# Mixture layer of a two-layer transformer: rows' low part moved from GpSimd to VectorE, normalising from VectorE to ScalarE

## What is computed

```
h = layernorm(x)                                   # (x - mean) / sqrt(var + eps), per row of 256
logits = (h @ router_w.T + router_b).reshape(T, O, E)
w, sel = top_k(softmax(logits, -1), 2); w = w / w.sum(-1)
c[t, e] = sum over o of the weights of expert e    # [T, 8]
out = sum over e of c[t, e] * (h @ expert_w[e].T + expert_b[e])
```

## Time and profile before

| | |
|---|---|
| median of 3 runs | 1158.56 us (1158.07 to 1158.87) |
| the profiled execution | 1155.52 us |
| its span | 1153.8 us |
| VectorE busy over the span | 854.3 us (74%) |
| TensorE, ScalarE, GpSimd busy | 981.7, 498.0, 307.6 us |
| the mixture layer | from about 287 to 597 us |

### The profile page before, as it was taken

One profiled execution on the slowest core, in us unless ns is written; L12 is line 12 of the kernel. 1 busy time (PEld: TensorE's weight loads), 2 busy tenths in 40 slices (PEclk: granted clock), 3 DMA queues, 4 the chain that ended last, 5 costly groups with the idle time before them and its releaser, 6 DMA issues. The chain is left out here.

```text
span 1153.8 us, 19875 instructions
## 1 busy us (share of the span) xinstructions
PE 981.7 (85%) x6885; PEld 579.3 (50%) x6960; DVE 854.3 (74%) x1556; ACT 498.0 (43%) x972; POOL 307.6 (27%) x337
## 2 busy tenths in 40 slices
PE   3698989897789778797649799999978999999997
PEld 1444545454446344454214366575846555656564
DVE  5677776651999999999977875858762776777766
ACT  2154444453465464564624433416131444444443
POOL 3234343441352432423321121304044400000000
PEclk9799999998899989798769999999988999999999
DMA  6622222200101001001000010101011000000000
GB/s 176 118 75 77 72 82 67 74 2 4 44 0 47 1 1 45 0 1 46 1 17 3 10 30 8 31 2 32 8 36 39 20 1 19 1 18 0 19 1 19
DMA packets 37087, 35.87 MB, mean 31 GB/s; under 512 B 8584, under 2 KB 33416, under 8 KB 37008
## 3 DMA queue, kind: packets, MB, share of 16 engines
q1 hardware_dynamic: 35728, 33.79, 10.5%
q10 hardware_dynamic: 1280, 1.05, 0.7%
HBM read 27.28 MB, written 6.29 MB: 29 GB/s over the span
## 5 line engine op out<-in xcount | busy, mean ns | idle before, releaser
L883 DVE TENSOR_REDUCE bm<-ps 128x4 f32<-128x512 f32 x160 | 102.1, 684 | 32.6 <-PE ps L603 30.5
L782 ACT ACTIVATE pt<-ps 128x1024 f32<-128x1024 f32 (+1 forms) x96 | 82.0, 882 | 70.9 <-PE ps L679 70.2
L2011 ACT ACTIVATE g<-ps 128x512 f32<-128x512 f32 x64 | 38.2, 597 | 134.4 <-PE ps L1958 107.4
L2061 DVE SCALAR_TENSOR_TENSOR g<-g,ps 128x512 f32<-128x512 f32 x64 | 44.0, 687 | 54.7 <-ACT g L2011 54.5
L1753 DVE TENSOR_TENSOR qk_lo<-ps,qk_hi 128x512 bf16<-128x512 f32 x80 | 54.8, 686 | 40.1 <-ACT qk_hi L1646 34.1
L599 PE MATMUL ps<-ks,qs 96*128 96x512 bf16 (+3 forms) x256 | 68.7, 323 | 11.9 <-DMA ks<-scratch_k 7.6
L156 POOL TENSOR_TENSOR mag_w<-stage 128x512 f32<-128x512 fp8e4 x24 | 26.4, 1100 | 191.2 <-DVE stage L143 191.2
L1515 PE MATMUL ps<-wp_hi,oT_hi 128*128 128x256 bf16 x256 | 71.2, 278 | 5.4 <-DVE oT_lo L1746 5.4
L547 POOL TENSOR_SCALAR_AFFINE_SELECT pt<-pt 128x256 f32<-128x256 f32 (+1 forms) x96 | 45.9, 484 | 109.4 <-ACT pt L782 108.9
L1974 PE MATMUL ps<-ew_hi,it_hi 128*128 128x256 bf16 x256 | 69.8, 273 | 6.0 <-DVE it_lo L2077 6.0
L1646 ACT ACTIVATE qk_hi<-ps 128x512 bf16<-128x512 f32 x80 | 48.1, 603 | 55.0 <-PE ps L1515 55.0
(11 more groups left out here) (272 smaller groups left out, 2803.5 us busy)
## 6 DMA issues: line engine op xcount, KB each, us to landing
qs<-scratch_q SPq DMA_DIRECT2D x64, 64.0 KB, 2.6
ks<-scratch_k SPq DMA_DIRECT2D x48, 64.0 KB, 2.5
q_next<-in_w_qkv SPq DMA_DIRECT2D x4, 768.0 KB, 5.0
X<-in_x SPq DMA_DIRECT2D x4, 512.0 KB, 7.0
w_next<-in_router_w SPq DMA_DIRECT2D x4, 512.0 KB, 3.9
w_next<-in_expert_w SPq DMA_DIRECT2D x4, 512.0 KB, 4.7
p_next<-in_w_proj SPq DMA_DIRECT2D x4, 512.0 KB, 5.9
out<-X SPq DMA_DIRECT2D x8, 256.0 KB, 2.3
```

Source lines behind the costliest of these rows:

```text
L782: act.activation(pt[kt][:, heads[0]:heads[-1] + 1, :], src, ACT.Exp).then_inc(s_exp, 1)
L883: ins = dve.tensor_reduce(bm[:, 2 * g + i // 5, 4 * (i % 5):4 * (i % 5) + 4], src.rearrange("p (k q) -> p k q", k=4), AX_X, ALU.max)
```

## The change

GpSimd's `tile_low` goes; VectorE gets it, for tile n+2, directly behind `weigh(n)` and ahead of the statistics and `from_second`. ScalarE's `tile_high` for tile n+2 comes directly behind `logits(n+2)` in every step that routes, and tiles 0 and 1 are done at the start. VectorE's `normalised` goes; ScalarE gets it at the head of tile 1's step, ahead of `logits`, in two steps: four times x + (-mean), then four times that times the root. GpSimd makes -mean (128x4) behind the root. `next_normalised`, for the next layer, stays on VectorE.

```diff
+        minus_mean = st.sb("minus_mean", [P, 4], F32)
+        s_centred, s_neg = st.sem("centred1"), st.sem("minus_mean")
...
 GpSimd
-                def tile_low(n, t):
-                    wait_alone(pool, s_xbhi, n + 1, passed_pool)
-                    pool.tensor_tensor(xb_lo[t % 2][:, :, :], xf[:, :, P * t:P * (t + 1)], xb_hi[t % 2][:, :, :],
-                                       ALU.subtract).then_inc(s_xblo, 1)
-                tile_low(0, 0)
                 from_middle(0, 0)
                 def batch(b, first, last):
                     for t, n, after, _ in tiles(b, last):
-                        if after and t != 2:
-                            tile_low(n + 1, after[1])
                         if after:
                             from_middle(n + 1, after[1])
                         if t == 0 and not last:
                             rstd_ops(pool, mv, rstd, half, s_mv, s_rstd, b + 1, passed_pool)
-                        if t == 1:
-                            tile_low(n + 2, 3)
+                            pool.tensor_scalar(minus_mean[:, :], mv[:, :, 0], -1.0, None, ALU.mult).then_inc(s_neg, 1)
...
 ScalarE
+                def normalised(b):
+                    act.wait_ge(s_rstd, 2 * b + 2)
+                    act.wait_ge(s_neg, b)
+                    for j in range(4):
+                        act.activation(xn[:, j, :], X[:, b, j, :], ACT.Identity, bias=minus_mean[:, j:j + 1]
+                                       ).then_inc(s_centred, 1)
+                    for j in range(4):
+                        act.wait_ge(s_centred, 4 * (b - 1) + j + 1)
+                        act.activation(xn[:, j, :], xn[:, j, :], ACT.Copy, scale=rstd[:, j:j + 1]).then_inc(s_xn, 1)
                 tile_high(0, 0, 0)
+                tile_high(0, 1, 1)
                 logits(1, 1)
                 def batch(b, first, last):
                     for t, n, after, routed in tiles(b, last):
-                        if after and t < 2:
-                            tile_high(after[0], n + 1, after[1])
-                        if t == 3 and not last:
-                            tile_high(after[0], n + 1, after[1])
+                        if t == 1 and not last:
+                            normalised(b + 1)
                         if routed:
                             logits(n + 2, routed[1])
-                        if t == 1:
-                            tile_high(b, n + 2, 3)
+                            tile_high(routed[0], n + 2, routed[1])
...
 VectorE
-                def normalised(b):
-                    dve.wait_ge(s_rstd, 2 * b + 2)
-                    for j in range(4):
-                        dve.tensor_scalar(xn[:, j, :], X[:, b, j, :], mv[:, j, 0:1], rstd[:, j:j + 1],
-                                          ALU.subtract, ALU.mult).then_inc(s_xn, 1)
+                def tile_low(n, t):
+                    dve.wait_ge(s_xbhi, n + 1)
+                    dve.tensor_tensor(xb_lo[t % 2][:, :, :], xf[:, :, P * t:P * (t + 1)], xb_hi[t % 2][:, :, :],
+                                      ALU.subtract).then_inc(s_xblo, 1)
                 two_greatest(0, 0)
+                tile_low(0, 0)
+                tile_low(1, 1)
                 from_second(0, 0)
                 def batch(b, first, last):
-                    for t, n, after, _ in tiles(b, last):
-                        if t == 1 and not last:
-                            normalised(b + 1)
+                    for t, n, after, routed in tiles(b, last):
                         weigh(b, n, t)
+                        if routed:
+                            tile_low(n + 2, routed[1])
                         if t == 0 and not last:
                             statistics(b + 1)
```

More of the change, by code:

```diff
@@ L1182, in token_weights @@
                                        ).then_inc(s_cw, 1)
+                act.sem_inc(s_xn, 4)
                 act.sem_inc(s_xhi, 4)
@@ L1225, in _ @@
                 dve.sem_inc(s_mv, 4)
-                dve.sem_inc(s_xn, 4)
                 dve.sem_inc(s_xlo, 2)
```

## The result

Eight runs of each kernel in turn gave a median of 1151.60 us (1149.59 to 1156.16) for the changed one against 1158.27 us for the one before; the ratio of their means is 0.9949, 95% interval 0.9932 to 0.9967. That is 5.9 us faster (3.8 to 7.9); the medians differ by 6.7. Two further comparisons, of 12 runs each, gave 0.9968 (0.9956 to 0.9981) and 0.9976 (0.9964 to 0.9988). The three intervals share only 0.9964 to 0.9967, some 4 us.

A forecast was written before the change was run, and what follows sets the result against it. The prediction took VectorE to bound the mixture stage. Its steps summed to -2.9 us, late logits made that -2.6, so from 1158.56 it forecast 1156.0 us, range 1153.0 to 1160.0.

The forecast's parts named there:

- start and (0,0): Start, and weighing tile 0 of batch 0: VectorE stands 2.5 us for ScalarE's copy, `wt` stall goes; +0.86 us.
- (0,2): Step weighing tile 2 of batch 0: VectorE's added low part, +0.34 us.
- (1,1): Step weighing tile 1 of batch 1: normalising leaves VectorE, ScalarE's copy comes last; -1.77 us.
- batch 2: All steps of batch 2, reckoned in the same way as batch 1, the last stall being 0.49; -1.60 us.
- (3,1): Step weighing tile 1 of batch 3: the low part stands for GpSimd's `wt`, about +0.6 us.
- late logits in (b,2): Tile 2's step of three batches: later transposes delay experts and router logits on TensorE; 0.1 us each.
- (b,1): Step weighing tile 1 of batch b, with ScalarE's eight normalising instructions at its start, taken as 3.2 us.
- T: Time mark in step (1,1): the end of VectorE's L1291, 401.03 us in the kernel before.
- rival D: Behind the stage: TensorE's granted clock gives back or doubles the gain; plus or minus 1.5 us, no chance of its own.
- Rival A: VectorE bound throughout, ScalarE's eight at 0.31 us each; some -4 us, 1154.6 us; chance 0.15.
- Rival B: Register work at the loop's low parts (+1.6) or late router logits eats the gain; -1 us, 1157.5; chance 0.30.
- Rival C: ScalarE's normalising becomes the bound in (b,1), each microsecond over 3.2 paid; table loads give 1163.7 us; chance 0.12.

The follow-up runs named there:

- low_twice: Changed kernel with each of VectorE's 16 low parts made twice, the first result unused; stage 312.21 us, one run of 1158.7 us.
- swap_only: Changed kernel with normalising left on VectorE, so only the low part moves; stage 310.51 us, ratio 1.0008 to the kernel before.
- act_longer: Changed kernel with four more unused ScalarE operations ahead of normalising in each of three steps; stage 312.38 us, one run of 1162.3 us.
- splits_early_stats: Changed kernel: next layer's weight split in ScalarE's idle time, copy ahead of logits for t = 0, statistics ahead of (3,1)'s low part; ratio 0.9909.
- after_again: The changed kernel measured once more with no edit; stage 306.74 us, ratio 0.9968 to the kernel before.
- copy_first: Changed kernel with ScalarE's row copy ahead of normalising and logits; stage 307.53 us, ratio 0.9988 to the kernel before.

## Why the prediction was right or wrong

By the steps of the sum, forecast against the two first traces:

| step | forecast | measured |
|---|---|---|
| start and (0,0) | +0.86 | +0.89 |
| (0,1) | -1.51 | -1.56 |
| (0,2) | +0.34 | +0.04 |
| (0,3) | -0.15 | -0.16 |
| (1,0), (1,1), (1,2), (1,3) | -0.02, -1.77, +0.34, -0.02 | -0.07, -1.89, +0.32, -0.02 |
| batch 2 | -1.60 | -1.79 |
| (3,0), (3,1) | -0.02, +0.61 | -0.03, +0.58 |
| late logits in (b,2) | +0.3 | nothing beyond the rows of (b,2) |
| sum | -2.6 | -3.70 |

**The mechanism of the stage held.** The bound is VectorE (low_twice), the swap is worth nothing by itself (swap_only: +0.7), the copy is last in (b,1) (act_longer: 1.6 us in, 1.6 us of waiting out), and the low part stands for `wt` in (3,1): splits_early_stats puts it behind the statistics, and it takes 0.39 us and not 1.01.

**One wait was sized wrongly.** The idle time behind `xb_hi` is 6.8 us in all, above the 5 us that the prediction named as a sign of being wrong. It had put 0.3 to 0.5 into each (b,1); the waits are 1.8, 1.1 and 1.1. In (1,1), where T is 397.12 now, VectorE was through weighing at 409.06, T+11.9, and not at T+12.7: the 0.75 us of stall beside GpSimd's root isn't there. The copy ended at T+13.0, as forecast (T+13.1), so this error turned into idle time and hardly touched the sum. Another 0.4 us of waiting is in (0,2).

**Sizes that were off.** (0,2): `wt` started 0.57 us behind L1278 where it had started 0.86 behind it, and the low part hides in that. (1,1) and (2,1) gave 0.12 us more each. The late logits that I priced at 0.3 make VectorE wait 0.37 us for the copy in (0,2) of the first trace, but the low part would have stood for `wt` there in any case, so they cost nothing. In after_again the waits of the steps (b,2) are 0.74, 0.27 and 0.38, where the first trace has 0.37, 0.12 and 0.12, and its stage is 0.5 us longer. Over its three traces the stage lost 3.1 to 3.6 us against the mean of before's two, where I forecast 2.6.

**The step that failed** is the plus or minus 1.5 us of rival D: "I put plus or minus 1.5 us on everything, no forecast of its own". It was worked out from no row, and D looked for the scatter behind the stage. It lies in front: the code there ends anywhere from 284.0 to 290.8 us in thirteen traces in which it is the same, and 35 runs of one kernel cover 6.5 us. Medians of eight runs drawn at random from these 35 fall between 1154.8 and 1158.2 in 95 of 100 draws (an estimate), and the difference of two such medians within 2.5 us. That also bears on the two numbers that the forecast started from: 1158.56, the median of three runs, stands 1.35 us above the median of the 35, 1157.21, and the 3.0 us between the profiled execution and the median were one draw of the same scatter, used as an offset (it is 2.0 for the changed kernel). If the 35 stand for the first measurement too, then of the 4.4 us between 1156.0 and 1151.6 some 1.4 are that start, some 1.1 the size of the gain (3.7 and not 2.6), and some 1.9 the luck of the first eight runs. The 3.7 us of the three comparisons together would have stood inside the range, 1153.0 to 1160.0; so would the medians of the two repetitions, 1153.6 and 1154.2.

**Rival A** (ScalarE's eight at 0.31 us) fell: they take 0.40. The Trainium skill ("ScalarE: Activation LUTs", section What ACT_TABLE_LOAD costs) puts 93 ns on each per-partition operand; the prediction's 0.31 without one and 0.09 are the 0.40 measured here. **Rival B** (waits eat it) fell as to register work: the low parts of the loop have 0.12 us in front of them, as L1285 had in the same place (0.13 at 415.75). Its other half, late logits in (b,2), shows in after_again and costs 0.5 us there, not 1.6. **Rival C** was the right place and the wrong side: each microsecond over 3.2 is paid, as act_longer shows, but they took 3.19, and Identity brought no table load (the stage has one, as before).

## What to carry to other kernels

When work leaves the engine that bounds a stage, ask which chain is next and how much shorter it is: here it was a copy on ScalarE, 1.1 us behind, and under it a second chain through TensorE, so the first repair (copy_first) gained nothing (its stage is 1.1 us longer). Taking unrelated work out of that chain gained 3.1 us in the steps (b,1), and the copy's new place another 2.5 in (0,0). Two parts of a change can be worth +0.7 and -2.0 alone and -3.4 together, so undoing one part doesn't price the other. Cut a trace at marks around the changed code before reading the total: the stage repeated within 0.5 us, the program only within 6.5. The scatter that goes into a forecast's range is to be measured first, by timing the kernel before against itself.

## What the runs showed of the hardware that I had not expected

A GpSimd operation doesn't always hold VectorE for as long as it runs. The root on 128x4 takes 1.04 us in the first layer, while VectorE copies from PSUM (kernel before):

```profile
217.86 1.04 POOL L524 TENSOR_TENSOR rstd<-rstd,half 128x4 f32<-128x4 f32 x1 [0.18 <-POOL rstd L522]
```

In the stage the same operation, L941, takes 2.95. It starts beside VectorE's L1290 and ends 0.9 us behind it, so it seems to wait for L1290 to end; but in these 0.9 us it runs beside L1265, which has two SBUF inputs and isn't stretched (1.22 us). `minus_mean`, 0.25 us beside L1266, doesn't stretch it either. The low part on GpSimd, 0.67 us on 128x256, cost VectorE 0.35 to 0.53. The Trainium skill ("SBUF — State Buffer", section SBUF: two separate sides) says that the one that starts first has the pair of ports for the whole instruction. For L1032, `wt` and the low part on VectorE (1.01 us in (3,1)) the traces agree, to within 0.15 us; for these two small operations they don't.
